# Row maxima of causal attention stored to memory in query order instead of partition order

## The reference, cut to what matters

```python
x = L0_attn_x                                   # (1, 2048, 256) float32
xn = layernorm(x)
k, q, v = W_K xn, W_Q xn, W_V xn                # 16 heads, head size 128
scores = einsum('biph,biqh->biqp', k, q)        # causal mask, -1e10 where masked
attn = softmax(masked / sqrt(128), axis=-1)     # over keys p
s = W_O . (attn v)                              # summed over heads
g = silu(base(xn) + routed_lora(xn))            # a small feed-forward part, at the end
out = x + s * g
```

## Time and profile before

| | |
|---|---|
| time, median of 3 runs | 1548.5 us (1548.2 to 1549.68) |
| the profiled execution's own time | 1548.1 us, span of the profile 1546.2 us |
| PE busy | 1459.5 us (94% of the span), 7788 matmuls |
| ACT busy | 1274.0 us (82%) |
| DVE busy | 1248.1 us (81%) |
| POOL busy | 793.4 us (51%) |
| granted TensorE clock, mean | 0.989 |

### The profile page before, as it was taken

One profiled execution on the slowest core, in us unless ns is written; L12 is line 12 of the kernel. 1 busy time (PEld: TensorE's weight loads), 2 busy tenths in 40 slices (PEclk: granted clock), 3 DMA queues, 4 the chain that ended last, 5 costly groups with the idle time before them and its releaser, 6 DMA issues.

```text
span 1546.2 us, 23204 instructions
## 1 busy us (share of the span) xinstructions
PE 1459.5 (94%) x7788; PEld 1193.2 (77%) x7788; DVE 1248.1 (81%) x2541; ACT 1274.0 (82%) x2196; POOL 793.4 (51%) x688
## 2 busy tenths in 40 slices
PE   5999999999999999999999999999999999999997
PEld 4877778777877878777787777877787777877765
DVE  6788877888788886888868887788878898788864
ACT  2788898889888898898988888888987988888962
POOL 2444655455465555456554555554645555544740
PEclk9899999999999999999999999999999999999998
DMA  2100010000100001000010001000010000100002
GB/s 75 49 8 14 15 25 25 15 15 8 29 21 15 15 7 42 15 14 13 10 42 15 7 15 28 22 15 14 8 35 21 15 7 13 40 8 15 15 28 82
DMA packets 30070, 33.75 MB, mean 22 GB/s; under 512 B 11008, under 2 KB 17664, under 8 KB 29952
## 3 DMA queue, kind: packets, MB, share of 16 engines
q1 hardware_dynamic: 29952, 32.26, 8.3%
HBM read 30.02 MB, written 2.23 MB: 21 GB/s over the span
## 4 chain that ended last, share of the span: by engine, by line
PE 51%; ACT 24%; DVE 13%; issue 9%; POOL 2%; DMA 0%; SPq 0%; ACTq 0%; POOLq 0%; DVEq 0%
PE ps L281 15%; PE ps L282 14%; PE ps L283 14%; ACT ps L478 7%; ACT probs L498 7%; ACT p_hi L499 6%; DVE p_lo L551 6%; PE ps L719 4%; DVE partmax L566 3%; POOL colsum L433 2%; PE ps L754 2%; ACT qT_hi L486 1%; DVE z_lo L588 1%; ACT z_hi L504 1%; PE ps L731 1%
## 5 line engine op out<-in xcount | busy, mean ns | idle before, releaser
L433 POOL TENSOR_TENSOR colsum<-colsum,probs 128x512 f32<-128x512 f32 (+3 forms) x512 | 610.2, 1192 | 388.3 <-ACT probs L498 373.6
L478 ACT ACTIVATE ps<-maxrow 128x512 f32<-128x512 f32 (+3 forms) x640 | 645.3, 1008 | 8.9 <-DMA maxrow<-max_dram 8.7
L551 DVE TENSOR_TENSOR p_lo<-probs,p_hi 128x512 fp32r<-128x512 f32 (+3 forms) x640 | 614.9, 968 | 42.4 <-ACT p_hi L499 41.4
L498 ACT ACTIVATE probs<-ps 128x512 f32<-128x512 f32 (+3 forms) x640 | 362.9, 567 | 141.4 <-PE ps L731 74.8
L499 ACT ACTIVATE p_hi<-ps 128x512 fp32r<-128x512 f32 (+3 forms) x640 | 365.3, 571 | 0.0
L566 DVE TENSOR_REDUCE partmax<-ps 128x1 f32<-128x512 f32 x384 | 256.9, 679 | 10.4 <-PE ps L719 9.5
L281 PE MATMUL ps<-qT_hi,kT_hi 128*128 128x512 f32 (+3 forms) x640 | 247.6, 387 | 12.7 <-ACT ps L478 9.6
L281 PE MATMUL ps<-p_hi,v_hi 128*128 128x512 f32 (+3 forms) x640 | 241.7, 378 | 13.2 <-DVE p_lo L551 12.2
L282 PE MATMUL ps<-qT_lo,kT_hi 128*128 128x512 f32 (+3 forms) x640 | 234.3, 366 | 0.0
L283 PE MATMUL ps<-qT_hi,kT_lo 128*128 128x512 f32 (+3 forms) x640 | 233.9, 366 | 0.0
L282 PE MATMUL ps<-p_lo,v_hi 128*128 128x512 f32 (+3 forms) x640 | 233.5, 365 | 0.0
(11 more groups left out here) (106 smaller groups left out, 2174.8 us busy)
## 6 DMA issues: line engine op xcount, KB each, us to landing
maxrow<-max_dram SPq DMA_DIRECT2D x64, 256.0 KB, 3.8
wraw<-wqk_dram SPq DMA_DIRECT2D x16, 256.0 KB, 3.8
acc<-x_dram SPq DMA_DIRECT2D x4, 512.0 KB, 7.2
wraw<-wv_dram SPq DMA_DIRECT2D x8, 256.0 KB, 4.7
wraw<-wo_dram SPq DMA_DIRECT2D x8, 256.0 KB, 2.9
probs<-x_dram SPq DMA_DIRECT2D x4, 512.0 KB, 4.5
out_dram<-acc SPq DMA_DIRECT2D x4, 512.0 KB, 3.0
max_dram<-rowmax SPq DMA_DIRECT2D x64, 2.0 KB, 1.4
```

The source lines that it names most:

```text
L433: nc.gpsimd.tensor_tensor(total[:, c0:], total[:, c0:], tile[:, c0:], ALU.add)\
L478: nc.scalar.activation(st[job.n % SCORE_BANKS].rearrange("p (t n) -> p t n", t=TB)[:, q:, :], maxrow[:, job.g, :].rearrange("p (n t) -> p ...
L498: nc.scalar.activation(probs[:, k, c0:], src, ACT.Exp, scale=SCALE).then_inc(probs_ready, 1)
L551: nc.vector.tensor_tensor(p_lo[:, k, c0:], probs[:, k, c0:], f32(p_hi[:, k, c0:]), ALU.subtract)\
```

## The change

The store writes the maxima in query order: the address of (p, t) is now 128 t + p. On the memory side the step from one partition to the next is one element and from t to t + 1 it is 128, so the four numbers of a partition no longer lie side by side. The broadcast read (line 345) is as before. The seed reads columns c0 and on of the row with step one; what it writes is the same as before, in place and in value.

```diff
-                    sp.dma_start(row.rearrange("(p t) -> p t", t=TB), rowmax[:, job.g, :]).then_inc(max_out, 16)
+                    sp.dma_start(row.rearrange("(t p) -> p t", p=P), rowmax[:, job.g, :],
+                                 allow_slow_non_contiguous=True).then_inc(max_out, 16)
                     sp.wait_ge(max_out, 16 * blocks)
...
-                q = columns(job) // P
-                nc.scalar.activation(st[job.n % SCORE_BANKS].rearrange("p (t n) -> p t n", t=TB)[:, q:, :],
-                                     maxrow[:, job.g, :].rearrange("p (n t) -> p t n", t=TB)[:, q:, :],
-                                     ACT.Copy, scale=-1.0).then_inc(seeded, 1)
+                c0 = columns(job)
+                nc.scalar.activation(st[job.n % SCORE_BANKS][:, c0:], maxrow[:, job.g, c0:], ACT.Copy, scale=-1.0)\
+                  .then_inc(seeded, 1)
```

## The result

The changed kernel takes 1788.8 us (median of 4 runs, 1785.17 to 1794.44), the kernel before 1548.35 (4 runs): ratio 1.156, 95% interval 1.152 to 1.159. The forecast was 1478, range 1450 to 1538. It is 240 us slower where 70 us were to be gained. The rival "the store of single elements is slow" is the one that came true, and beyond its own price of 1574.

What follows compares the result with a forecast made beforehand. The prediction took TensorE (PE, 94% busy) as the bound, with stalls partly from ACT's slow seed. 1548.1 less 70 us for the seed, store cost of at most 4 us allowed for in the 70, gave 1478 us, range 1450 to 1538.

Steps and rivals of the forecast that it cites:

- the store of single elements is slow: Rival on the maxima store: landing grows by 4.2 us to 5.6, total 1574 us; chance 0.08, of which 0.05 slower.
- the 282 of the sum: ACT's busy time: cheaper wide and narrow seeds at exponential prices take about 282 us off, 1274 to some 992.
- the 0.55 us: Seed of 512 in place on ACT: holds the next instruction 1.03 us, a step-one copy 0.48, so 0.55 saved.
- the step is not the cause: Rival on the seed: reading SBUF or writing PSUM sets the price, seed stays 1155 ns, 1548 to 1552 us; chance 0.09.
- ceiling of 115 from PE's dense rate: PE stalls: a pair needs 168 us of matmuls in 182.4, so some 14 us a pair, 115 us in all, can be gained.
- the 91 of the chain: Seeds on the chain, at L478 and behind issue: halving them shrinks the old chain by 56 to 91 us, 91 close to a cap.
- the lower half: Seed's gain taken as 70 us from 56 to 91, since other paths, above all DVE's, come to the fore.
- The rival that DVE eats the gain: Rival on PE's waits for DVE: only 25 us gained, 1523 us; gain of 4 to 50 us given chance 0.23.
- I take 0.7: Store's landing: 512 pieces instead of 128 make it 0.7 us longer, at most 4 us in all.
- an upper bound of 4.2: Store's landing: if all 1.4 us grows with the piece count it is 5.6, so 4.2 us more.
- the rival's 1.3 of slack and 1.4 of lead: Slow-store rival: of 4.2 us a block, 1.3 is slack before the first seed, 1.4 covered by the two-tile lead.
- slower by a slow store: The part of the slow-store rival in which the changed kernel ends slower; chance 0.05.

Runs made afterwards that it cites:

- the seed alone: Changed kernel's step-one seed with the store of the kernel before; 1448.98 us, ratio to before 0.936.
- step two: Store of before; full-width seeds read the row with step two instead of four, narrow ones with step one; 1443.28 us in one run.
- the adjoining pieces: Step-one seed, store of before, plus a second store of side-by-side 4-byte pieces to memory nobody reads; 128 pieces 1678 us, 256 pieces 1623 us.
- Two stores in a row: Step-one seed and the store of before made twice, the second issued when the first has landed; 1458.28 us.
- The hop on chip: Step-one seed; the 512 small pieces go first to one on-chip partition, then one contiguous store to memory; 1482.63 us, ratio 0.956.
- 4-byte pieces in place: Step-one seed; store of 512 pieces of 4 bytes to the addresses of before; 1645.84 us, ratio 1.063.

## Why the prediction was wrong, point by point

**The seed: right.** The step was the cause: 612 ns against the 642 forecast, so 543 ns saved on a seed where 510 were counted. ACT's busy time still fell by 240 us and not by the 282 of the sum. The sum added lengths of records, and neighbours on ACT overlap; the 0.55 us that the prediction read from the places on the engine gives 448 x 0.55 = 246 for the wide seeds, and ACT lost 246 with the seed alone (1274.0 to 1027.6). The fit is rough, since the narrow seeds and the exponentials got shorter too. The rival "the step is not the cause" is gone. Of the Trainium skill's page "SBUF — State Buffer", section "Door 1: The DMA port swizzle", the runs agree with the line of 16 bytes and the two hits on it (step two, 657 ns against 612); its "free" stride of 4 fp32 they refute (1155 ns).

**What the seed is worth: 99 us, not 70.** The ceiling of 115 from PE's dense rate held; the 91 of the chain, called close to a cap, was passed. To take the lower half for DVE's sake was the error. With the seed alone ACT and PE's waits on DVE nearly vanish from the chain (PE 93%, DVE 5%), so DVE had mostly been late because ACT was, as far as the chain tells. The exponentials, too, went from 642 to 602 ns, some 2 x 448 x 0.04 = 36 us in summed lengths of ACT's records, which no step had foreseen; why they got shorter stays open. The rival that DVE eats the gain is refuted.

**The store: the step that failed.** "I take 0.7, since most of the 1.4 us is not moving of data", and an upper bound of 4.2 from a landing in proportion to the count. The count and the moving were as told (packets under 512 B went from 11,008 to 35,584, just 24,576 more, which agrees with the one descriptor per element of the Trainium skill's page "DMA: Bandwidth & Descriptors", section "Rules for kernel authors"). But the part held constant, from the last piece moved to the landing, grew from 0.4 to 7 us. Between the issue of the store and that of the read it is 7.0 more in all (8.43 at 556.86 against 1.44 at 503.40 in the earlier trace rows, which are also the medians of the 64 blocks): a landing of 8.4 us, where the sum had 2.1 and the upper bound 5.6. It depends on how many pieces lie close together in memory, of which the trace of before has only one case, and neither bound was built on it. The read behind it was held to be as before; it takes 4.7 us in place of 3.8 in the changed kernel, and 3.1 when the row was stored in 128-byte pieces. The slower read goes with the row that is read, not with any late store ahead of it: where the adjoining pieces went to the unread memory, the read took 3.4 us (128 pieces) and 3.3 (256).

**What hides it, and the price of the rival.** A block's row is 7.0 + 0.9 = 7.9 us late. Over 64 blocks this is 506 us, of which 340 were lost against the seed alone. Taken together, 2.6 us a block were hidden, next to the rival's 1.3 of slack and 1.4 of lead, 2.7 in sum. Two stores in a row, 2 us, cost 9 us. The hop on chip, with 3.6 us more from the first store to the read (5.02 against 1.44) and a read that is 0.6 quicker, makes the row 3.0 late and cost 34. From there to the changed kernel a further microsecond a block costs (340 - 34) / (7.9 - 3.0) = 62 us, about one for each of the 64 blocks, the lower clock included. The mechanism of the rival was right, its landing was not: with 4.2 the price was 1574.

That its 2.7 of slack fits so well is partly luck. Of the 340 us, PE's idle time (span less busy) is (1784.5 - 1519.2) - (1448.5 - 1412.8) = 230, or 3.6 a block, so 4.3 of the 7.9 us were hidden from PE. The rest, 1519.2 - 1412.8 = 106, is the same matmuls at a lower clock: by windows of 0.5 us over the whole span PE is busy for 225 us at a granted clock of 0.50 in the changed kernel and for 14 with the seed alone, and half of the difference is 106. The prediction had no term for the clock, and this cost made up for slack that it had counted too small.

**The chance.** 0.05 for "slower by a slow store" was too little for an operation that the trace did not show once, in a chain in which one block of each pair had no slack, and with the rule on strided last dims in the Trainium skill's page "DMA: Bandwidth & Descriptors", section "Rules for kernel authors", against it.

## What to carry to other kernels

A layout change moves its price from the engine that reads to the one that writes: here 543 ns on each of 448 seeds went into 7 us on each of 64 stores, and 64 serial waits won. Before scattering small elements side by side to outer memory, turn them on chip so that neighbours in memory are neighbours on a partition; one 0.21 us instruction of VectorE and four stores of 128-byte pieces gave the whole gain. And the landing of a DMA is not its moving: bound an unseen pattern by a run of its own, not by scaling the landing of another.

## What the runs showed of the hardware beyond expectation

- Adjoining 4-byte writes to outer memory land late: 6.5 to 8.5 us for 128 to 512 of them, against 2.3 us for 512 that are 64 bytes apart and 1.8 us for 256 in pairs 64 bytes apart. With on-chip memory as the target, adjoining pieces land 1.6 us after the issue on average.
- The broadcast read of 256 KB takes 4.7 us when its row was just written in scattered 4-byte pieces, 4.1 in 4-byte pieces in place, 3.8 in 16-byte pieces and 3.1 in 128-byte pieces. Late 4-byte writes to other memory ahead of it do not slow it (3.3 and 3.4).
- After an idle stretch of 5.7 us TensorE worked at a granted clock of 0.50 for 5.4 us. Over the whole changed kernel such stretches cost 106 us.
- ScalarE reads 512 columns of SBUF with step four in 1155 ns, with step two in 657, with step one in 612 to 619.
